# Message-passing and expert kernel: expert rows weighted on VectorE and added into the output by DMAs, and a third row buffer for the last window

## What is computed

```python
x = x + gnn(layernorm(x))                 # 6 steps, 3125 nodes x 256
xf = layernorm(x)
logits = xf @ Wg + bg + bias              # 8 experts
topk_vals, topk_idx = top_k(logits, 2)
topk_w = softmax(topk_vals)
combine = (one_hot(topk_idx, 8) * topk_w[..., None]).sum(axis=1)
h = relu(einsum('td,edh->teh', xf, W1) + b1)      # 256 -> 512
y = einsum('teh,ehd->ted', h, W2) + b2            # 512 -> 256
return x + einsum('ted,te->td', y, combine)
```

## Time and profile before

| | |
|---|---|
| median of 3 runs | 2170.54 us (2167.09 to 2171.59) |
| profiled execution | 2174.05 us, span 2172.3 us |
| PE busy | 1908.7 us, 88% of the span |
| DVE busy | 1098.8 us, 51% |
| ACT busy | 593.5 us, 27% |
| POOL busy | 309.2 us, 14% |
| expert loop, first to last POOL DMA into `chosen_out` | 1952.1 to 2134.3 us of the span |
| end of the span | 2172.3 us |

### The profile page before, as it was taken

The page is one execution under the profiler, slowest core; times in us unless marked ns, Lnnn a source line. Parts: engine busy times, 40 slices in busy tenths (PEclk is TensorE's granted clock), DMA queues, the critical chain, the costliest instruction groups (busy, mean ns, idle before and its releaser), DMA issues.

```text
span 2172.3 us, 31473 instructions
## 1 busy us (share of the span) xinstructions
PE 1908.7 (88%) x11126; PEld 1132.8 (52%) x11127; DVE 1098.8 (51%) x2464; ACT 593.5 (27%) x1268; POOL 309.2 (14%) x434
## 2 busy tenths in 40 slices
PE   1667776999999999999999999999999999749991
PEld 1533334445654457444564456544574456549991
DVE  6589992245533455244442445344452556625555
ACT  0145552122222123212231222221231112126660
POOL 0013324554000000000000000000000022323331
PEclk7679998999999999999999999999999999869996
DMA  8900004443000000000000000000000001632225
GB/s 266 336 23 0 0 0 144 141 133 110 1 2 1 1 1 1 2 1 1 1 2 1 1 1 1 2 1 1 1 1 1 1 25 35 286 128 86 87 79 192
DMA packets 74393, 113.64 MB, mean 52 GB/s; under 512 B 10635, under 2 KB 63670, under 8 KB 73233
## 3 DMA queue, kind: packets, MB, share of 16 engines
q1 hardware_dynamic: 56618, 52.49, 8.1%
q0 software_dynamic: 12736, 39.29, 5.3%
q10 hardware_dynamic: 4902, 20.01, 2.3%
HBM read 49.99 MB, written 61.77 MB: 51 GB/s over the span
## 4 chain that ended last, share of the span: by engine, by line
PE 69%; DVE 15%; issue 8%; POOL 4%; ACT 1%; DMA 1%; SPq 1%; ACTq 0%; POOLq 0%; another core or an unknown queue 0%; DVEq 0%
PE bank L1403 36%; PE bank L1427 25%; DVE hot_key L760 6%; PE bank L1387 4%; POOL chosen_out L564 3%; DVE hot_row L754 2%; PE bank L1382 1%; PE bank L1301 1%; SPq L439 1%; DMA slot_in<-x_rows,slot_of 1%; DMA y_pair<-chosen_out 0%; PE bank L1329 0%; PE bank L1471 0%; PE bank L1275 0%; DVE r_lo L820 0%
## 5 line engine op out<-in xcount | busy, mean ns | idle before, releaser
L1403 PE MATMUL bank<-adj,r_lo 128*128 128x512 fp8e4 (+2 forms) x2100 | 729.9, 352 | 0.0
L1403 PE MATMUL bank<-adj,r_hi 128*128 128x512 fp8e4 (+2 forms) x2100 | 729.9, 352 | 0.0
L1403 PEld LDWEIGHTS bank<-adj,r_hi 128*128 128x128 f16 x2100 | 205.6, 98 | 189.4 <-issue 0.8
L1403 PEld LDWEIGHTS bank<-adj,r_lo 128*128 128x128 f16 x2100 | 205.5, 98 | 189.5 <-issue 0.8
L827 DVE SCALAR_TENSOR_TENSOR m_lo<-bank,msg_unit,m_hi 128x512 f16<-128x512 f32 (+2 forms) x84 | 57.2, 682 | 309.3 <-ACT m_hi L1113 309.2
L538 POOL TENSOR_TENSOR rstd<-rstd,expo 128x4 f32<-128x4 f32 (+1 forms) x7 | 6.8, 972 | 1309.1 <-DVE rstd L913 1309.1
L1329 PE MATMUL bank<-hot_key,hot_row 128*128 128x400 f16 x588 | 142.3, 361 | 57.1 <-DVE hot_key L760 54.8
L1427 PE MATMUL bank<-m_hi,wct_hi 128*128 128x512 f16 (+2 forms) x504 | 177.3, 352 | 0.0
L1427 PE MATMUL bank<-m_lo,wct_hi 128*128 128x512 f16 (+2 forms) x504 | 177.3, 352 | 0.0
L1427 PE MATMUL bank<-m_hi,wct_lo 128*128 128x512 f16 (+2 forms) x504 | 177.3, 352 | 0.0
L1427 PE MATMUL bank<-x_hi,wht_lo 128*128 128x512 f16 (+2 forms) x504 | 177.3, 352 | 0.0
(11 more groups left out here) (287 smaller groups left out, 2940.0 us busy)
## 6 DMA issues: line engine op xcount, KB each, us to landing
slot_in<-fill_rows SPq DMA_DIRECT2D x2, 13520.0 KB, 69.1
ffn_scratch<-pair POOLq DMA_DIRECT2D x32, 512.0 KB, 3.2
ffn_w<-ffn_scratch ACTq DMA_DIRECT2D x8, 2048.0 KB, 16.0
x_rows<-in_L_ffn_W POOLq DMA_DIRECT2D x32, 256.0 KB, 3.9
slot_x<-slot_in SPq DMA_DIRECT2D x30, 260.0 KB, 2.7
y_pair<-chosen_out SPq DMA_DIRECT2D x8, 640.0 KB, 9.0
xa<-in_x SPq DMA_DIRECT2D x1, 3072.0 KB
x<-in_x ACTq DMA_DIRECT2D x1, 3072.0 KB
```

What stands on the lines that cost most here:

```text
L1403: last = mm(bank[f][:, 0:n], r[:, q, f * P:(f + 1) * P], c, start=q == 0 and i == 0, stop=q == NT - 1 and i == len(todo) - 1)
```

## The change

1. `output` on DVE writes bias + product into a new buffer `y_sum` (which frees bank 5 for PE by a semaphore of its own, `y_read`), computes the row's weight (`share`: from exp(v1 - v0), which travels as a third extra column of the row), and multiplies `y_sum` by it into one of two buffers `slot_y[j]`, one per half tile.
2. POOL sends each half by an indirect DMA that adds into `out` (`compute_op=ALU.add`, rows with a destination over N-1 are dropped), with a semaphore `y_out{j}` for each half. POOL waits for landings only at the end of each expert; DVE waits for `y_out{j}` of the tile before, ahead of writing `slot_y[j]`.
3. `x1` is stored to `out` by SP window by window in the last step; POOL waits for these stores before the first adding DMA. The read back, the sums on DVE and the stores at the end are gone.
4. ACT computes exp(v1 - v0) of each tile (`exp_now`) ahead of `xt_hi`; the weights' instructions after `place(NW-1)` are gone. DVE keeps the difference per window (`diff_kept`).
5. The last window has its own row buffer, slot buffer and semaphore (`own(w)`). `x_end` and `hid_bias_rows` move into other buffers' space; POOL therefore clears the row buffers after `hid_bias_t`.

```diff
-        x2_rows = [lb(f"x2_rows{i}", [P, 4, ROW], F32) for i in range(2)]
+        x2_rows = [lb(f"x2_rows{i}", [P, n, ROW], F32) for i, n in enumerate((4, 4, WIN_TILES[-1]))]
...
+        def own(w):
+            return w % 2 if w < NW - 1 else 2
+
         def scattered_by(w):
-            return 16 * 2 * sum(WIN_TILES[w % 2:w + 1:2])
+            return 16 * 2 * sum(WIN_TILES[v] for v in range(w + 1) if own(v) == own(w))
...
-            sp.wait_ge(sem("rows"), rows_before(NW))
+            for w in range(NW):
+                t0, t1 = WIN_T0[w], WIN_T0[w] + WIN_TILES[w] - (w == NW - 1)
+                sp.wait_ge(sem("x1_sum"), rows_before(w + 1))
+                sp.dma_start(out[t0 * P:t1 * P, :].rearrange("(t p) d -> p t d", p=P), x1[:, t0:t1, :]).then_inc(sem("stored"), 16)
+            sp.dma_start(out[(NT - 1) * P:N, :], x1[0:TAIL, NT - 1, :]).then_inc(sem("stored"), 16)
...
             sp.wait_ge(sem("experts_done"), 1)
-            G = NT // FIN
-            for g in range(FIN):
-                for k in range(2):
...
-            sp.wait_ge(sem("stored"), 16 * (FIN + 1))
...
-            for i in range(2):
-                pool.memset(x2_rows[i][:, :, D + 2:ROW], 0.0).then_inc(sem("rows_clear"), 1)
+            pool.wait_ge(sem("hid_bias_t"), 1)
+            for i in range(3):
+                pool.memset(x2_rows[i][:, :, D + 3:ROW], 0.0).then_inc(sem("rows_clear"), 1)
...
+            pool.wait_ge(sem("stored"), 16 * (NW + 1))
             pool.wait_ge(sem("tiles_of"), 1)
+            for j in range(TT):
+                pool.dma_start(started[j:j + 1, :].rearrange("a p -> p a"), valid[:], allow_slow_non_contiguous=True).then_inc(sem(f"y_out{j}"), 16)
...
-                    pool.wait_ge(sem("y_ready"), 2 * n + 4)
-                    pool.tensor_tensor(tick[:], valid[:], valid[:], ALU.mult).then_inc(sem("ticks"), 1)
                     for j in range(TT):
-                        pool.indirect_dma_start(chosen_out[:], bass.IndirectOffsetOnAxis(ap=dest[:, j:j + 1], axis=0),
-                                                slot_y[:, j, :], None).then_inc(sem("y_out"), 16)
-                    pool.wait_ge(sem("y_out"), 16 * TT * n + 16 * TT)
-                    pool.tensor_tensor(tock[:], valid[:], valid[:], ALU.mult).then_inc(sem("y_sent"), 1)
+                        pool.wait_ge(sem("ticks"), TT * n + (j + 1))
+                        pool.wait_ge(sem(f"y_ready{j}"), n + 2)
+                        pool.tensor_tensor(tick[:, j:j + 1], valid[:], valid[:], ALU.mult).then_inc(sem("ticks"), 1)
+                        pool.indirect_dma_start(out[:], bass.IndirectOffsetOnAxis(ap=dest[j][:, 0:1], axis=0), slot_y[j][:], None,
+                                                bounds_check=N - 1, oob_is_err=False, compute_op=ALU.add).then_inc(sem(f"y_out{j}"), 16)
                     pool.reg_add(done, done, 1)
+                for j in range(TT):
+                    pool.wait_ge(sem(f"y_out{j}"), pool.snap(pool.snap(done) * 16 + 16))
+                    pool.tensor_tensor(tock[:, e * TT + j:e * TT + j + 1], valid[:], valid[:], ALU.mult).then_inc(sem("expert_sent"), 1)
...
-                v.tensor_copy(kept, slot_x[:, :, D:D + 2]).then_inc(sem("meta_kept"), 1)
+                v.tensor_copy(kept[:, :, 0:2], slot_x[:, :, D:D + 2])
+                v.tensor_copy(kept[:, :, 2], exp_now[:]).then_inc(sem("meta_kept"), 1)
...
             def output(e, n):
-                dve.wait_ge(sem("y_sent"), n + 1)
                 dve.wait_ge(sem("y_part"), HT * n + 2 * HT)
-                v.tensor_tensor(slot_y[:], bank[5][:].rearrange("p (j d) -> p j d", j=TT), out_bias[:, e:e + 1, :].broadcast_to([P, TT, D]), ALU.add)                 .then_inc(sem("y_ready"), 1)
+                for j in range(TT):
+                    dve.wait_ge(sem(f"y_ready{j}"), n + 1)
+                v.tensor_tensor(y_sum[:], bank[5][:].rearrange("p (j d) -> p j d", j=TT), out_bias[:, e:e + 1, :].broadcast_to([P, TT, D]), ALU.add)\
+                 .then_inc(sem("y_read"), 1)
...
+                v.tensor_scalar(total[:], meta_now[:, :, 2], 1.0, None, ALU.add).then_inc(sem("dest_part"), 1)
+                v.scalar_tensor_tensor(share[:], meta_now[:, :, 1], float(e), meta_now[:, :, 2], ALU.is_equal, ALU.max).then_inc(sem("dest_part"), 1)
+                dve.wait_ge(sem("dest_part"), DEST_OPS * n + 2)
+                v.reciprocal(total[:], total[:]).then_inc(sem("dest_part"), 1)
+                dve.wait_ge(sem("dest_part"), DEST_OPS * n + 4)
+                v.tensor_tensor(share[:], share[:], total[:], ALU.mult).then_inc(sem("dest_part"), 1)
+                dve.wait_ge(sem("dest_part"), DEST_OPS * n + 5)
+                dve.wait_ge(sem("y_read"), n + 2)
+                for j in range(TT):
+                    dve.wait_ge(sem(f"y_out{j}"), 16 * n + 16)
+                    v.tensor_copy(dest[j][:], meta_now[:, j, 0:1])
+                    v.tensor_scalar(slot_y[j][:], y_sum[:, j, :], share[:, j:j + 1], None, ALU.mult).then_inc(sem(f"y_ready{j}"), 1)
...
             def tile_hi(n):
                 act.wait_ge(sem("turned"), n + 2)
+                a.activation(exp_now[:], slot_x[:, :, D + 2], ACT.Exp)
                 a.activation(xt_hi[:].rearrange("p t n -> p (t n)"), bank[4][:], ACT.Copy).then_inc(sem("tile_hi"), 1)
...
             def layer2(e, n):
-                pe.wait_ge(sem("y_ready"), 2 * n + 2)
+                pe.wait_ge(sem("y_read"), n + 1)
```

More of the change, by code:

```diff
@@ L68 @@
 TT = TILE // P
+DEST_OPS = 5
 CAP = (N + TILE - 1) // TILE * TILE
@@ L227, in gnn_ffn @@
         bs.close()
+        x_end = [m[:, NW % 2].rearrange("p t n -> p (t n)").bitcast(F32) for m in (m_hi, m_lo)]
         late = ExitStack()
@@ L283, in gnn_ffn @@
         slot_x = fb("slot_x", [P, TT, ROW], F32)
-        slot_y = fb("slot_y", [P, TT, D], F32)
+        slot_y = [fb(f"slot_y{j}", [P, D], F32) for j in range(TT)]
         xt_hi = fb("xt_hi", [P, DT, TILE], F32R)
         xt_lo = fb("xt_lo", [P, DT, TILE], F32R)
-        meta = fb("meta", [P, MAX_TILES + 2, TT, 2], F32)
-        meta_now = fb("meta_now", [P, TT, 2], F32)
-        dest_f = fb("dest_f", [P, TT], F32)
-        dest = fb("dest", [P, TT], U32)
-        tick = fb("tick", [P, 1], F32)
-        tock = fb("tock", [P, 1], F32)
+        meta = fb("meta", [P, MAX_TILES + 2, TT, 3], F32)
+        meta_now = fb("meta_now", [P, TT, 3], F32)
+        exp_now = fb("exp_now", [P, TT], F32)
+        total = fb("total", [P, TT], F32)
+        share = fb("share", [P, TT], F32)
+        y_sum = fb("y_sum", [P, TT, D], F32)
+        dest = [fb(f"dest{j}", [P, 1], U32) for j in range(TT)]
+        tick = fb("tick", [P, TT], F32)
+        tock = fb("tock", [P, NX * TT], F32)
         ended = fb("ended", [P, 1], F32)
@@ L541, in scatter @@
                 pool.wait_ge(sem("slot_of"), w + 1)
+                pool.wait_ge(sem("diff_kept"), w + 1)
                 for t in range(WIN_TILES[w]):
@@ L1503, in all_steps @@
                 pe.wait_ge(sem("gate_in"), 64)
-                nc.tensor.transpose(bank[2][:, 0:BLOCKS], hid_bias_rows[:], ident[0:BLOCKS, 0:BLOCKS]).then_inc(sem("hid_bias_t"), 1)
+                nc.tensor.transpose(bank[2][:, 0:BLOCKS], hid_bias_rows, ident[0:BLOCKS, 0:BLOCKS]).then_inc(sem("hid_bias_t"), 1)
                 pe.wait_ge(sem("iotas"), 13)
```

85 lines of the change are left out of this document (25 added, 60 removed).

## The result

| | median us | lowest to highest | profiled span |
|---|---|---|---|
| before | 2170.95 | 2167.09 to 2171.59 (4 runs) | 2172.3 |
| changed | 2137.51 | 2134.63 to 2137.68 (4 runs) | 2135.8 |

The ratio is 0.9846, with a 95% interval of 0.983 to 0.9861: 33.4 us faster. Forecast were 42.2, with a range that held the result. The profiled execution of before was a long one of its kind, so the two spans lie 36.5 us apart.

The account below looks back on a forecast made before the run. PE, busy 88% of the span, bounds the kernel; gains lie where it doesn't work. End -33.2, loop -6, front -3.3, small things +0.3 give -42.2 us: median 2170.54 becomes 2128.3, range 2122 to 2146.

Parts of the forecast that it names:

- End at 2139.1 ... -33.2 us: Program end: without read back, sums and stores the span ends at 2139.1 in place of 2172.3 us, -33.2 us.
- SP then only leaves, 0.2 + 0.45 us: Very end: after `ended` at 2138.4 only SP's leaving remains, 0.2 + 0.45 us.
- +0.9: Last tile: the chain from DVE's bias sum to POOL's first `tick` takes 2.1 us, not 1.25, so +0.9 us.
- I take +1.0: Last landing: the adding DMA's read of its destination adds 1.0 us to a plain landing of 1.53 us.
- The front ... -3.3: Before the expert loop: the last `normalise` no longer waits for window 4's scatters, -3.3 us (-3.8 to 0).
- rival 3: The front gives nothing, since last scatters queue behind weights and stores: 2131.6 us; chance 0.1 together with rival 4.
- rival 4: The wait for window 4 only moves to SP; same time as rival 3, chance 0.1 together with it.
- I take -6: Expert loop: PE's 7.7 us of waits for DVE's `dest` mostly go, -6 us (bounds -7.7 to +8).
- Rival 2: The adding DMA is slow: landing above 4.2 us costs the loop, 5.7 us uses up the gain; chance 0.08.
- Rival 1: New loop waits replace the old: loop gives 0 to +10, not -6, about 2141 us; chance 0.2.
- SP's load: Loop: the tile load is issued 0.45 us later; in time at 2.7 us landing, costs 0.5 us at 4.0.
- small things: Row buffers cleared later, between PE and DVE, +0.3 us (0 to +0.8); the other small items 0.

Follow-up runs that it names:

- the early DMAs: The changed kernel with the two `started` DMAs moved ahead of the row scatters on POOL's queue; 2133.32 us, ratio 0.9838 to before.
- before with 64 bytes: The kernel before, with only the weights of experts 0 to 5 placed 64 bytes further in SBUF; ratio 0.9983 to before.
- the joined halves: The changed kernel with POOL waiting for both written halves and DVE for both landings before either half; 2190.5 us, ratio 1.0077 to before.
- the rows shared: The changed kernel with `started` DMAs ahead of the scatters and the last window sharing an earlier window's row buffer; ratio 0.9831 to before.

## Why the prediction was right or wrong

The direction and the cause were right: the read back, sums and stores left the path, PE's waits for DVE left the loop, and the range held. The sum was 9 us too good, and it was luck that it wasn't more: 3.4 us of the gain come from where the weights lie, which no step had. Without them the miss would be 12 us. The steps:

**"End at 2139.1 ... -33.2 us": 25.9, the step that failed.** The forecast's own tail was 41.85 - 33.2 = 8.65 us; measured are 15.97. By its terms:
- "SP then only leaves, 0.2 + 0.45 us": SP did, but POOL's drain ends the span 5.9 us after `ended` begins: +5.1 with it. It was in the trace of before, 5.5 us long under the read back. I had read what lay last and not what the removed work covered. The move of the wait to DVE shows that it starts once POOL's last work is done; no run made the drain itself shorter.
- "+0.9" for the chain up to the first `tick`: the chain's own instructions are about the 2.1 us forecast (1.9 in the first tile, 1949.2 to 1951.1, with `reciprocal` of 2 columns 0.17 and not 0.35), but `tick` came 4.4 us after the bias sum, since the last expert has one tile and POOL first waits for both landings of the expert before: +2.3. The margin was worked out for a period of 6.17 us; the last period is 4.13.
- POOL's part: an adding issue is 0.56 us longer, twice: +1.3 with the `tick`. The forecast priced the addition at the landing alone.
- "I take +1.0" for the landing: 1.2 us from the end of the issue, not 2.5: -1.3. In the loop the addition adds 0.5 us.

2.3 + 1.3 - 1.3 + 5.1 = 7.4 us, against 15.97 - 8.65 = 7.3 unrounded. The bound "-29" of this step is a slip too: with +4 for the landing in place of +1 its sum gives -30.2.

**"The front ... -3.3": the buffer's gain was real, and given back.** By the four kernels with and without it the buffer brings 2.4 to 2.9 us. But "the two `started` DMAs ... lie between POOL's last scatter ... and its first DMA of the loop at 1952.1, where POOL has no other work ...: 0" named POOL's idle time as the cover and forgot who waits for what stands ahead on its queue: SP waited for the scatters' landing, and these DMAs held it up, by 4.2 us in the profiled pair and by 4.8 and 5.3 us in the two pairs of experiments. So the sign came that the forecast had named for being wrong, "a front that still begins at 1928". The front gave nothing, as rival 3 said, but by another mechanism; rival 4 (the wait only moves to SP) is what the trace looks like, and what the early DMAs refute. In the profiled pair 1.6 us came back from PE's clock, below, which is no gain of the change.

**"I take -6" for the loop: -9.3, of which -5.9 by the step.** PE's 7.7 us for DVE went as forecast. Rival 2 did not come: the median landing is 3.8 us from the start of the issue, 2.25 from its end, and the longest 5.2 and 3.65, below the 4.2 and 5.7. (Rival 2's "about 2197" leaves the loop's -6 in the sum beside its +64.) Rival 1 came in small: DVE's `dest` did wait for the DMAs and PE for `slot_x`, which the forecast had named as its sign, but they cost some 2 us and not 6 to 16. The margin that gave way was the one for "SP's load". The other 3.4 us of the 9.3 are the shifted weights: before with 64 bytes gains the same 3.4 with none of the change. "The loop's period is 6.17 us throughout" was wrong for that reason. How little room the margins left is shown by the joined halves: the same DMAs behind one wait make the kernel 1.0077 of before.

7.3 of the end, -3.3 of the loop and 1.7 of the front (with the 0.3 of small things) are the 5.7 us between the forecast for the profiled pair, -42.2, and its -36.5. The medians lie 33.4 apart, because the profiled execution of before was 3 us above its median.

## What to carry to other kernels

Before removing the work at the end of a program, look under it: what each engine still does there, its drain too, becomes the end, and the last tile has a shorter period than the margins of the loop. A DMA costs not only its issue and landing but what lands behind or before it on the same queue, so small DMAs of single elements belong where nobody waits. A wait that the engine on the path doesn't show can still reach it through the next load. And when a change resizes buffers, look where the hot operands went: the same pitch of PE before and after tells whether a gain is the change's own.

## What was not expected of the hardware

- POOL's drain takes 5.1 to 6.0 us from the end of its last instruction in all 14 profiles, with a DMA outstanding or not.
- An adding indirect DMA of 128 rows of 1 KB is issued in 1.55 us, a plain one in 0.99. The last two scatters of the front, of 53 rows, also take 1.55 us and are plain. Their packets are 13 of 4160 bytes in a row, one of 1040 and 195 of 16 bytes, where a scatter of 128 rows has 32 of 4160; whether that is why they take longer to issue is open.
- A pair of DMAs of 128 four-byte elements holds up the landing of the scatter ahead of it: 11.0 to 12.1 us from its issue to the load in the seven kernels that have it there, 6.7 to 6.8 in the other seven. As one row each it doesn't. Most of it lies in one packet of the scatter, of 3.7 to 4.6 us; why was not tried further.
- Float32 matmuls of the same shape take 277 or 282 ns by where their operands start in SBUF (durations with modelled ends; start to start it is 114 or 119).
- From the first tile load to the first bias sum pass 20.4 to 20.9 us in seven of the fourteen profiles and 22.05 to 23.2 in the other seven, for the same work. The granted clock (the last but two of a row's values) tells them apart. With the `started` DMAs early, then with them early and the rows shared:

```profile
1919.00:1941.00 22.00, 14.07 (x101) 13.46 (x102) 6.32 (x20) 9.32 (x24) 0.00 (x0) 0.79 0.19 50
```

```profile
1924.00:1948.00 24.00, 16.14 (x94) 15.54 (x95) 5.57 (x18) 8.72 (x23) 0.00 (x0) 0.68 0.17 43
```

PE had nothing to do before the first tile came. A mean of 0.79 between the levels 1.2 and 2.4 GHz is 12.8 of 22 us at the upper one, 0.68 is 8.6 of 24. Before and changed fell into different groups (22.05 us with a granted clock of 0.71, 20.50 with 0.79), but the changed front has members in both (20.87 and 20.69, 22.66 and 23.16), as has before's (20.70 with 64 bytes more), so I don't put these 1.6 us down to the change. What decides it stays open.
